# A two-layer graph-attention kernel: unroll factor 4 to 8, a power in place of Newton steps, and a second attention with transposed scores, fp32 probabilities in column tiles and a mask added by TensorE

## The chip, the cores and the metric

The kernel runs on one core of one Trainium2 chip. The metric is the device time of one execution in microseconds. The core has TensorE (PE for its matmuls, PEld for its weight loads), VectorE (DVE), ScalarE (ACT), GpSimd (POOL) and SyncE (SP, which issues the transfers). Each engine runs its own list of instructions and waits for the others on semaphores.

## What is computed

64 graphs (batches) of 256 nodes with 256 features each go through two graph-attention layers with 8 heads of 32 dimensions. Cut to what matters:

```
# layer 0
q, k = src @ Wq + bq, src @ Wk + bk
attn = softmax(q @ k.T / sqrt(32))                      # per head
out = sum over r in 0..3 of (attn * (adj == r)) @ (src @ Wv[r] + bv[r])
x = layernorm(src + out @ Wo + bo)                      # g1, beta1
x = layernorm(x + gelu(x @ W1 + b1) @ W2 + b2)          # the feed-forward
# layer 1
q, k, v = x @ Wq, x @ Wk, x @ Wv
e = q @ k.T ; e = where(e >= 0, e, 0.2 * e)             # per head, leaky
attn = softmax(where(adj > 0, e, -9e15))
h = layernorm(attn @ v)
out = layernorm(concat(h, x) @ Wffn.T) + x
```

A row of `adj` without any edge has all its scores at -9e15, so its softmax is uniform.

## The kernel before

A batch is two tiles of 128 nodes. The kernel has three stages, one after the other, each with a barrier at its end and with its results in DRAM: `attention_first` (names with `a_`), `feed_forward` (`f_`, on pairs of batches) and the second attention, `attention_layer` with layer 1 (`l_`). Between the first two stands a general form of layer 0, which runs only where `adj` has values other than 0 and 1.

**How a stage is ordered.** The engines' lists are written by hand as a software pipeline. `run_steps` (L68) calls `step(t)` for one batch after the other: first 2·U of them written out, then a loop `Fori(2, B // U)` (L74) whose body holds U batches, then a tail. U is 4, so eight batches are written out and the loop runs 14 times four. The feed-forward does the same with pairs (L1644), in 6 loop passes. A step has eight slots, one for each head; a table `AT` says in which slot, counted from the batch's first, each part of a batch's work is put, so that a step holds work of several batches at once. Where two parts fall into one slot, the order of the code in `step` decides.

**First attention.** It forms the transposed scores and needs no transposes of P. Per batch: projections with fp16 high and low parts (three products for each, L1456 to L1458), store of q and k to a scratch in DRAM and six loads into a `stack` whose 96 rows hold the three high/low combinations, the scores (L1485) for the row maxima, the maxima turned and stored and loaded as two more rows of the stack (98 rows), transposed scores with the maximum already subtracted (L1472), the exponential on ScalarE (L1211) to fp32 `prob`, and value products in fp32 whose results, 32 rows each, lie in four column tiles of TensorE at once (L1547, L1550). Per batch, one turn of the negative maxima stands on TensorE (L1558). GpSimd makes the low part `a_xl` of the next input (L1303) after ScalarE's high part `a_xh` (L1227), and the low part `a_hl` of the heads (L1294), for which TensorE's output projection waits. The layernorm's reciprocal root is, after the variance, a seed on VectorE (with the negated mean five small operations) and three Newton steps of four operations on [128 x 2] on GpSimd (L1323), then the shift (L1326).

**Second attention.** Per head and batch: TensorE makes the scores (L909) and adds the mask, a bf16 product with the identity (L912), for each of the two node tiles; ScalarE makes the leaky part (a relu scaled by 4, L473, one pass of 512 columns), VectorE joins it with the scores and finds the row maximum in the same pass (L726, two of 256 columns), ScalarE makes the exponentials with their row sums (L433, two of 256), TensorE transposes the fp32 P (L896, four), ScalarE copies its high part (L446), VectorE subtracts for the low part (L732), and TensorE multiplies with the values in twelve products of 32 columns (L813 to L815). Around the heads stand the projections, `l_qk` with its low parts (L698), its store and eight loads into `l_stack` for each batch, two layernorms by the same Newton steps, and the output projection, copied to `l_y` (L792).

## Time and profile before

| | |
|---|---|
| median of three runs | 3583.69 us |
| the three runs | 3582.01 to 3592.45 us |
| the profiled execution | 3597.16 us |
| its span | 3594.9 us |
| first attention | 0 to 1244 us |
| feed-forward | 1244 to 1990 us |
| second attention | 1990 to 3595 us |
| busy share of the span | TensorE 86% (weight loads 64%), VectorE 76%, ScalarE 68%, GpSimd 49% |
| mean granted clock of TensorE | 0.944 of full speed |

The profile is of one execution. The stage borders are where the names of the instructions change. An engine's busy share over the span is a mean over three stages with different limits, so the views below are taken by stage. TensorE's records overlap, since a matmul enters the engine while the one before leaves it: the distance from one start to the next tells what a matmul costs, its own duration doesn't. PEclk is the granted clock as a share of full speed. The queue rows (PEldq, SPq) are control instructions, as the branch at a loop's end.

### The profile page before, as it was taken

The page shows a single profiled execution, that of the slowest core. Times are in us where ns is not written, and L with a number is a line of the kernel's source. Part 1 is how long each engine was busy: PE and PEld are TensorE (multiplying, and loading weights), DVE is VectorE, ACT ScalarE, POOL GpSimd, SP SyncE. Part 2 cuts the span into 40 slices and gives each one's busy share as a digit, 9 for nine tenths or more (in the row PEclk, how much of TensorE's full clock was granted, in tenths as well). Part 3 has the DMA queues.
Part 4 walks back from the last instruction along what each step waited for, and adds up shares of the span by engine and source line. Part 5 has one row for each costly group of instructions (what it writes and reads, how often), then busy time and mean ns, then how long its engine had stood idle before and what let it go on. Part 6 is the DMA issues. An engine that isn't in the chain of part 4 may idle for free. (4 is left out here: it accounts for less than half of the span.)

```text
span 3594.9 us, 96982 instructions
## 1 busy us (share of the span) xinstructions
PE 3085.4 (86%) x31169; PEld 2287.0 (64%) x31169; DVE 2723.2 (76%) x7645; ACT 2427.9 (68%) x5646; POOL 1769.1 (49%) x3716
## 2 busy tenths in 40 slices
PE   5999999999999489999999488878888888788886
PEld 3666666666665256666666377767777777677775
DVE  4888888888888345655555388888888888888886
ACT  2566666666666255555555488888888888888886
POOL 0566666666666425545545034443444444344445
PEclk9999999999999789999999699998999999999998
DMA  3444444444444111111111344443443444344332
GB/s 117 131 133 132 132 132 132 132 132 132 132 132 124 42 47 48 54 52 47 47 47 38 94 113 115 118 114 102 114 119 103 112 115 115 100 113 119 106 109 60
DMA packets 296923, 364.46 MB, mean 101 GB/s; under 512 B 29536, under 2 KB 213728, under 8 KB 296544
## 3 DMA queue, kind: packets, MB, share of 16 engines
q1 hardware_dynamic: 295104, 358.20, 33.6%
q8 instruction: 185, 3.03, 0.4%
q14 instruction: 194, 1.59, 0.2%
q10 hardware_dynamic: 1440, 1.65, 0.1%
HBM read 241.77 MB, written 117.96 MB: 100 GB/s over the span
## 5 line engine op out<-in xcount | busy, mean ns | idle before, releaser
L433 ACT ACTIVATE l_prob<-l_neg_e,l_neg_max 128x256 f32<-128x256 f32 x1024 | 518.0, 522 | 18.0 <-DVE l_neg_max L726 10.2
L726 DVE CUSTOM_DVE_ANT_0 l_neg_e<-l_score,l_leaky 128x256 f32<-128x256 f32 x1024 | 391.7, 420 | 151.0 <-ACT l_prob L433 93.1
L896 PE MATMUL l_tprob<-l_ident,l_prob 128*128 128x128 f32 x2048 | 362.3, 304 | 157.8 <-ACT l_prob L433 146.8
L473 ACT ACTIVATE l_leaky<-l_score 128x512 f32<-128x512 f32 x512 | 307.6, 601 | 219.8 <-PE l_score L912 219.6
L1774 DVE TENSOR_TENSOR f_gl<-f_act,f_gh 128x512 f16<-128x512 f32 x256 | 244.9, 957 | 275.5 <-ACT f_act L1701 275.4
L909 PE MATMUL l_score<-l_stack 128*128 128x256 f16 x1024 | 283.3, 299 | 107.0 <-DMA l_stack<-qk_scratch 106.9
L1696 ACT ACTIVATE f_gh<-f_up,f_b 128x512 f16<-128x512 f32 x256 | 175.5, 685 | 279.1 <-PE f_up L1822 279.0
L1387 DVE TENSOR_TENSOR a_linked<-a_prob,a_mask 128x1024 f32<-128x1024 f32 x256 | 350.2, 1368 | 6.9 <-ACT a_prob L1211 6.9
L732 DVE TENSOR_TENSOR l_pt<-l_tprob,l_pt 128x512 f16<-128x512 f32 x512 | 351.1, 686 | 1.4 <-ACT l_pt L446 1.4
L896 PEld LDWEIGHTS l_tprob<-l_ident,l_prob 128*128 128x128 f32 x2048 | 235.9, 151 | 174.7 <-ACT l_prob L433 130.2
L543 POOL TENSOR_TENSOR l_hl<-l_zt,l_hh 128x512 f16<-128x512 f32 x64 | 74.0, 1156 | 507.6 <-ACT l_hh L493 507.6
L1380 DVE TENSOR_REDUCE a_neg_max<-a_score 128x4 f32<-128x1024 f32 x256 | 307.3, 1200 | 4.1 <-PE a_score L1485 4.1
L1211 ACT ACTIVATE a_prob<-a_score_t 128x1024 f32<-128x1024 f32 x256 | 259.6, 1014 | 74.9 <-PE a_score_t L1472 73.4
L446 ACT ACTIVATE l_pt<-l_tprob 128x512 f16<-128x512 f32 x512 | 309.0, 604 | 1.0 <-PE l_tprob L896 1.0
L912 PE MATMUL l_score<-l_mask,l_identb 128*128 128x256 bf16 x1024 | 283.7, 299 | 0.0
L1820 PE MATMUL f_down<-f_w,f_gh 128*128 128x256 f16 x1024 | 279.2, 273 | 1.0 <-DVE f_gl L1774 1.0
L1822 PE MATMUL f_down<-f_w,f_gl 128*128 128x256 f16 x1024 | 279.1, 273 | 0.0
L1821 PE MATMUL f_down<-f_w,f_gh 128*128 128x256 f16 x1024 | 279.1, 273 | 0.0
L1432 DVE SCALAR_TENSOR_TENSOR a_qk<-a_proj,a_vcol,a_qk 128x256 f16<-128x256 f32 x256 | 112.1, 480 | 144.6 <-ACT a_qk L1220 144.5
L814 PE MATMUL l_heads<-l_vl,l_pt 128*128 128x32 f16 x2048 | 208.5, 178 | 12.1 <-issue 12.1
L433 ACT ACTIVATION_READ_ACCUMULATOR l_prob<-l_neg_e,l_neg_max 128x1 f32 x1024 | 218.2, 213 | 0.0
L813 PE MATMUL l_heads<-l_vh,l_pt 128*128 128x32 f16 x2048 | 211.3, 179 | 0.8 <-DVE l_pt L732 0.8
(227 smaller groups left out, 10376.2 us busy)
## 6 DMA issues: line engine op xcount, KB each, us to landing
l_stack<-qk_scratch SPq DMA_DIRECT2D x512, 128.0 KB, 3.1
a_stack<-qk_scratch SPq DMA_DIRECT2D x384, 128.0 KB, 2.8
qk_scratch<-a_qk SPq DMA_DIRECT2D x64, 512.0 KB, 2.8
qk_scratch<-l_qk SPq DMA_DIRECT2D x64, 512.0 KB, 4.7
a_x_sb<-x_t SPq DMA_DIRECT2D x64, 256.0 KB, 2.7
a_adj_sb<-adj_t SPq DMA_DIRECT2D x64, 256.0 KB, 2.8
a_res<-x_nodes SPq DMA_DIRECT2D x64, 256.0 KB, 3.0
after_attention<-a_z_out SPq DMA_DIRECT2D x64, 256.0 KB, 2.1
```

Source lines behind the costliest of these rows:

```text
L433: last = nc.scalar.activation(prob[:, s, i], src[:, i], ACT.Exp, bias=neg_max[:, s, i:i + 1], scale=1.0 if first else -1.0, accum_out=rsum ...
L446: nc.scalar.activation(pt[:, ht % PTB, 0], tprob[s][:], ACT.Copy).then_inc(pt_high, 1)
L473: nc.scalar.activation(leaky4[:, s], score[s][:], ACT.Relu, scale=1.0 / ALPHA - 1.0).then_inc(relu_done, 1)
L726: last = nc.vector.tensor_tensor_reduce(neg_e[:, s, i], score[s][:, i], leaky4[:, s, i], -ALPHA, 3e38, ALU.add, ALU.min, neg_max[:, s, i:i ...
L732: nc.vector.tensor_tensor(pt[:, ht % PTB, 1], tprob[s][:], pt[:, ht % PTB, 0], ALU.subtract).then_inc(pt_low, 1)
L896: last = nc.tensor.transpose(tprob[s][:, jt, it * P:(it + 1) * P], prob[:, s, it, jt * P:(jt + 1) * P], ident[:])
L909: last = nc.tensor.matmul(score[s][:, it], stack[:, i, 0, a, c * N + it * P:c * N + (it + 1) * P], stack[:, i, 1, a, c * N:(c + 1) * N], s ...
L912: last = nc.tensor.matmul(score[s][:, it], identb[:], mask[:, i, it * N:(it + 1) * N], start=False, stop=True)
L1380: nc.vector.tensor_reduce(neg_max[:, i, 0:MROWS].rearrange("p (a c t) -> p c a t", a=HQ, c=DC)[:, c, a0:a0 + 2], score[:], AX_X, ALU.max, ...
L1387: nc.vector.tensor_tensor(linked[:, k], prob[:, k], mask[:, be[1] % 2].unsqueeze(1).to_broadcast([P, 2, NT * N]), ALU.mult).then_inc(link_ ...
L1820: nc.tensor.matmul(out, lhs_h, rhs_h, start=start, stop=False)
L1821: nc.tensor.matmul(out, lhs_h, rhs_l, start=False, stop=False)
```

## The change

1. **U from 4 to 8.** 16 batches (or pairs) are written out ahead of each loop, the body holds 8, and the loop runs 6 times (2 times in the feed-forward). `attention_first` keeps its four buffers by a constant of its own, so its waits and transfers keep their distances.
2. **The reciprocal root** in all stages: VectorE makes only var + eps and the negated mean (three small operations fewer), GpSimd raises to -0.5 (one operation on [128 x 2]) and makes the shift. The wait that guards the root's buffer moves from VectorE to GpSimd.
3. **A new second attention**, `attention_second` (names with `b_`), built like the first:
   - The scores of each head are made twice. Once as before with the mask added (one bf16 product of 512 columns), only for the row maximum, which VectorE takes in one plain pass of 512 columns.
   - Once transposed, in PSUM `score_t`: two products of 256 columns; ScalarE replaces them in place by 4·relu; TensorE adds the mask `far` times 5·(-9e15) (one bf16 product of 512 columns) and the scores once more, this time with the two rows that subtract the maximum (two products of 256); ScalarE makes exp(0.2·x) in one pass of 512 columns to fp32 `prob`, which lies already as the values need it.
   - Values and sums by fp32 products in four column tiles, as in the first attention. The sums are turned and inverted by VectorE.
   - The maximum goes through one transpose, two small VectorE operations, a store and a load per batch.
   - Nodes without edges: `linked` (VectorE, from the transposed adjacency), a count by TensorE, `any_link` (VectorE), `zero_q` (VectorE, one product over q's both parts, 1024 columns), `far` (GpSimd). Both forms of the adjacency are loaded for each batch, 256 KB each, where there was one.
   - The x-part of the output projection (`out_x`) runs on the kept `xh`, `xl`; layernorm's scale and shift are folded into the weights and one row, so the output is `y = bank + out_row`.

```diff
-U = 4
-RSQRT_MAGIC = float(0x5F3759DF)
-NEWTON = 3
+U = 8
...
-                        n = 0
-                        for _ in range(NEWTON):
-                            for out, a, c, op in ((s["prod"], s["half"], s["root"], ALU.mult), (s["prod"], s["prod"], s["root"], ALU.mult),
-                                                  (s["prod"], s["prod"], three_halves, ALU.add), (s["root"], s["root"], s["prod"], ALU.mult)):
-                                nc.gpsimd.tensor_tensor(out[:], a[:], c[:], op).then_inc(root_chain, 1)
-                                n += 1
-                                pool.wait_ge(root_chain, count(bg, ROOTS, n))
+                        if (n := after(back(bg, 1), 1, 1)) is not None:
+                            pool.wait_ge(z_ready, n)
+                        nc.gpsimd.tensor_tensor(s["root"][:], s["var"][:], minus_halves[:], ALU.pow).then_inc(root_chain, 1)
+                        pool.wait_ge(root_chain, count(bg, ROOTS, 1))
                         nc.gpsimd.tensor_tensor(shift[:], s["neg_mean"][:], s["root"][:], ALU.mult).then_inc(root_chain, 1)
...
+def attention_second(nc, x_in, x_out, adj, adj_t, w, scr, scr_m, consts):
...
+    AT = {"load": 4, "load_adj": 4, "xT": 8, "xh": 9, "xl": 9, "q": 10, "q_hi": 11, "q_lo": 11, "linked": 8, "k": 12, "k_hi": 13, "k_lo": 13,
+          "count": 9, "any": 9, "v": 14, "v_out": 15, "zero_q": 12, "far": 10, "store_qk": 13, "mask": 16, "S": 17, "max": 17,
+          "offset": 24, "turn_max": 25, "max_rows": 26, "store_m": 26, "ST": 28, "relu": 28, "add": 29, "exp": 29, "values": 33, "res": 45,
+          "evac": 40, "turn_sum": 40, "rinv": 41, "turn_heads": 43, "hs": 43, "stats0": 44, "z1": 45, "turn_z": 46, "hh": 46, "hl": 47,
+          "out_x": 47, "out": 48, "y": 49, "stats1": 50, "z": 52, "affine": 53, "store": 55}
...
+                        sp.dma_start(scr[i].rearrange("k p n -> p k n"), qk[:, i]).then_inc(qk_stored[i], 16)
+                        sp.wait_ge(qk_stored[i], parts_stored)
...
+                        for blk, (kq, kk) in enumerate(((0, 2), (1, 2), (0, 3))):
+                            for which, kind in ((0, kq), (1, kk)):
+                                sp.dma_start(stack[DH * blk:DH * (blk + 1), r4, which],
+                                             scr[i, kind].rearrange("(a r) n -> r a n", r=DH)).then_inc(stack_loaded[r4], 16)
...
+                        act.wait_ge(added, head_count(be, he))
+                        if he % HQ == 0 and (n := after(back(be, 1), HALVES, 2 * (he // HQ) + 2)) is not None:
+                            act.wait_ge(values_done, n)
+                        nc.scalar.activation(prob[:, he], score_t[s][:].rearrange("p t n -> p (t n)"), ACT.Exp,
+                                             scale=ALPHA).then_inc(exp_done, 1)
...
+                        act.wait_ge(scores_t_done, head_count(br, hr))
+                        nc.scalar.activation(score_t[s][:], score_t[s][:], ACT.Relu, scale=SLOPE - 1.0).then_inc(relu_done, 1)
...
+                        nc.vector.tensor_reduce(neg_max[:, i, col:col + NT], score[s][:], AX_X, ALU.max, negate=True).then_inc(max_done, 1)
...
+                        pe.wait_ge(relu_done, head_count(be, he))
+                        if he == 0:
+                            pe.wait_ge(max_loaded[r4], uses(be, RING) * 16)
+                            pe.wait_ge(far_ready, count(be, 1, 1))
+                        nc.tensor.matmul(score_t[s][:].rearrange("p t n -> p (t n)"), far_ident[:], far[:, r4].rearrange("p t n -> p (t n)"),
+                                         start=False, stop=False, skip_group_check=True)
+                        for jt in range(NT):
+                            last = nc.tensor.matmul(score_t[s][:, jt], stack[0:KS, r4, 1, a, c * N + jt * P:c * N + (jt + 1) * P],
+                                                    stack[0:KS, r4, 0, a, c * N:(c + 1) * N], start=False, stop=True, skip_group_check=True)
+                        last.then_inc(added, 1)
...
+                        for term in range(2):
+                            for a in range(HQ):
+                                he = HQ * c + a
+                                part = slice(DH * a, DH * (a + 1))
+                                if term:
+                                    last = nc.tensor.matmul(sums_t[part, 0:N], pick[:, c], prob[:, he, cols], start=k == 0, stop=k == 3)
+                                else:
+                                    nc.tensor.matmul(heads_t[part, c], values[:, r4, jt, he * DH:(he + 1) * DH], prob[:, he, cols],
+                                                     start=jt == 0, stop=jt == 1)
...
-    attention_layer(nc, 1, mid2, out, adj, w1, scr1, consts)
+    attention_second(nc, mid2, out, adj, adj_t, w1, scr1, scr_m, consts)
```

**What stands on TensorE for a head of the second attention, before.** In one slot of the loop: `l_tprob` takes the transposed P of one head, `l_score` the scores and mask of a later head, and `l_heads` the values of an earlier one (four rounds of three, two shown).

```order
L896 MATMUL l_tprob<-l_ident,l_prob 128x128 x4
L909 MATMUL l_score<-l_stack 128x256
L912 MATMUL l_score<-l_mask,l_identb 128x256
L909 MATMUL l_score<-l_stack 128x256
L912 MATMUL l_score<-l_mask,l_identb 128x256
L813 MATMUL l_heads<-l_vh,l_pt 128x32
L814 MATMUL l_heads<-l_vl,l_pt 128x32
L815 MATMUL l_heads<-l_vh,l_pt 128x32
L813 MATMUL l_heads<-l_vh,l_pt 128x32
L814 MATMUL l_heads<-l_vl,l_pt 128x32
L815 MATMUL l_heads<-l_vh,l_pt 128x32
```

After, in one slot, with the buffer numbers: `b_score_t0` is completed for one head, `b_score_t1` begun for the next, `b_score0` made for the maximum of a later batch; `b_back_bank` holds turned maxima and the count.

```order
L2091 MATMUL b_score_t0<-b_far,b_far_ident 128x512
L2094 MATMUL b_score_t0<-b_stack 128x256 x2
L2103 MATMUL b_score_t1<-b_stack 128x256 x2
L2113 REGISTER_ALU
L2115 MATMUL b_score0<-b_stack 128x256 x2
L2117 MATMUL b_score0<-b_mask,b_identb 128x512
L2187 MATMUL b_back_bank<-b_ident,b_offset 128x128
L2190 REGISTER_ALU
L2194 MATMUL b_back_bank<-b_linked,b_ones 128x256 x2
L2214 MATMUL b_heads_t<-b_prob,b_values 32x256 x4
L2212 MATMUL b_sums_t<-b_prob,b_pick 32x256 x4
```

The transposes of P are gone. The second addition into `b_score_t0` stands first in the slot and waits for ScalarE's relu of a product that was issued one slot earlier; the products of the next head's `b_score_t1` stand right behind it. One quarter of a batch's values stands in every other slot.

**What stands on GpSimd in the first attention before `a_xl`, before.** The last of the three Newton steps, the shift and the low part of the next input:

```order
L1323 TENSOR_TENSOR a_nw_prod<-a_nw_half,a_nw_root 128x2
L1323 TENSOR_TENSOR a_nw_prod<-a_nw_prod,a_nw_root 128x2
L1323 TENSOR_TENSOR a_nw_prod<-a_nw_prod,a_three_halves 128x2
L1323 TENSOR_TENSOR a_nw_root<-a_nw_root,a_nw_prod 128x2
L1326 TENSOR_TENSOR a_shift<-a_nw_neg_mean,a_nw_root 128x2
L1303 TENSOR_TENSOR a_xl<-a_x_sb,a_xh 128x512
```

After:

```order
L1303 TENSOR_TENSOR a_nw_root<-a_nw_var,a_minus_halves 128x2
L1305 TENSOR_TENSOR a_shift<-a_nw_neg_mean,a_nw_root 128x2
L1285 TENSOR_TENSOR a_xl<-a_x_sb,a_xh 128x512
```

One power stands where twelve operations stood; `a_xl` and what follows it, up to `a_hl`, keep their order.

## Rows read from the trace of the kernel before

**Rows 1.** Stages: us; busy PE, PEld, DVE, ACT, POOL (xcount); PEclk; DMA share; GB/s.

```profile
0.00:1244.00 1244.00, 1123.90 (x11713) 706.49 (x11713) 1012.33 (x1747) 698.82 (x1285) 762.44 (x1284) 0.99 0.40 124
1244.00:1990.00 746.00, 699.25 (x4864) 479.49 (x4864) 414.47 (x899) 419.17 (x707) 354.88 (x512) 0.97 0.15 49
1990.00:3595.00 1605.00, 1262.26 (x14592) 1101.00 (x14592) 1296.36 (x4999) 1309.93 (x3654) 651.79 (x1920) 0.90 0.39 108
```

**Rows 2.** One line's instructions: count: least/mean/most ns, first to last start; shapes.

```profile
L1558 PE MATMUL a_sums_t<-a_ident,a_neg_max x53: 327/328/332, 215.4 to 1149.3; 128*128 128x128 f32 x53
...
L792 DVE COPY l_y<-l_back_bank x4: 680/680/681, 2281.2 to 2350.0; 128x512 f32<-128x512 f32 x4
...
L792 DVE COPY l_y<-l_back_bank x49: 678/680/682, 2281.2 to 3441.9; 128x512 f32<-128x512 f32 x49
...
L1485 PE MATMUL a_score<-a_stack x1024: 270/272/422, 45.4 to 1173.3; 96*128 96x256 f16 x171
```

**Rows 3.** Loop branches on TensorE's queue, in the three stages; columns as before.

```profile
L74 PEldq COMPARE_BRANCH  x14: 76/208/234, 209.9 to 1143.8; - x14
...
L1644 PEldq COMPARE_BRANCH  x6: 76/208/230, 1504.7 to 1939.0; - x6
...
L74 PEldq COMPARE_BRANCH  x13: 3469/3819/3950, 2262.5 to 3422.7; - x13
```

**Rows 4.** Timeline of two first-attention batches: start us, us, engine, line, [idle <-releaser].

```profile
598.84 0.62 ACT L1227 ACTIVATE a_xh<-a_x_sb 128x512 f16<-128x512 f32 x1
...
599.62 1.16 POOL L1303 TENSOR_TENSOR a_xl<-a_x_sb,a_xh 128x512 f16<-128x512 f32 x1
...
613.47 0.20 POOL L1323 TENSOR_TENSOR a_nw_prod<-a_nw_half,a_nw_root 128x2 f32<-128x2 f32 x1 [1.43 <-DVE a_nw_root L1425]
...
616.45 0.62 ACT L1227 ACTIVATE a_xh<-a_x_sb 128x512 f16<-128x512 f32 x1
...
617.33 0.20 POOL L1323 TENSOR_TENSOR a_nw_root<-a_nw_root,a_nw_prod 128x2 f32<-128x2 f32 x1
...
617.77 1.17 POOL L1303 TENSOR_TENSOR a_xl<-a_x_sb,a_xh 128x512 f16<-128x512 f32 x1
```

**Rows 5.** Waits, 200:1100 and 2200:3400: engine, its work <- releaser: us, times, longest.

```profile
PEld a_back_bank L1456 <- POOL a_hl L1294: 50.3, 50, 1.4
...
PE l_score L909 <- DMA l_stack<-qk_scratch: 80.0, 45, 2.5
```

**Rows 6.** Timeline of TensorE in the first attention, columns as in rows 4.

```profile
600.77 0.66 PE L1563 MATMUL a_back_bank<-a_ident,a_rinv_wide 128*128 128x128 f32 x4
601.26 0.60 PE L1472 MATMUL a_score_t<-a_stack 98*128 98x256 f16 x4
601.70 0.38 PE L1456 MATMUL a_proj<-a_wn,a_xh 128*128 128x512 f16 x1
601.92 0.38 PE L1457 MATMUL a_proj<-a_wn,a_xh 128*128 128x512 f16 x1
...
603.00 0.60 PE L1485 MATMUL a_score<-a_stack 96*128 96x256 f16 x4
603.53 0.64 PE L1550 MATMUL a_heads_t<-a_prob,a_values 128*32 128x256 f32 x8
...
604.42 0.61 PE L1547 MATMUL a_sums_t<-a_prob,a_pick 128*32 128x256 f32 x8
604.97 0.61 PE L1472 MATMUL a_score_t<-a_stack 98*128 98x256 f16 x4
```

**Rows 7.** Group by shape, 2200:3400: xcount | busy us, mean ns | idle before.

```profile
L473 ACT ACTIVATE l_leaky<-l_score 128x512 f32<-128x512 f32 x397 | 238.1, 600 | 170.3 <-PE l_score L912 170.2
```

**Rows 8.** DMA issues of the whole run: xcount, KB each, median us to landing.

```profile
l_stack<-qk_scratch SPq DMA_DIRECT2D x512, 128.0 KB, 3.1
...
qk_scratch<-a_qk SPq DMA_DIRECT2D x64, 512.0 KB, 2.8
qk_scratch<-l_qk SPq DMA_DIRECT2D x64, 512.0 KB, 4.7
```

More of the change, by code:

```diff
@@ L78, in run_steps, with norm_scratch @@
         step((B // U + r // U, r % U))
-def newton_scratch(ctx, nc, name, n):
-    return {k: ctx.enter_context(nc.sbuf_tensor(f"{name}_{k}", [P, n], I32 if k == "bits" else F32))
-            for k in ("var", "half", "bits", "root", "prod", "neg_mean")}
+def norm_scratch(ctx, nc, name, n):
+    return {k: ctx.enter_context(nc.sbuf_tensor(f"{name}_{k}", [P, n], F32)) for k in ("var", "root", "neg_mean")}
 def attention_layer(nc, layer, x_in, x_out, adj, w, scr, consts, other_edges=None, general=False):
@@ L204, in attention_layer @@
         shift = [sb(f"shift{i}", [P, NT], F32) for i in range(2)]
-        nw = [newton_scratch(ctx, nc, f"{L}nw{i}", NT) for i in range(2)]
+        nw = [norm_scratch(ctx, nc, f"{L}nw{i}", NT) for i in range(2)]
         score = [psum(f"score{i}", [P, NT, N]) for i in range(2)]
@@ L1065, in attention_first @@
         prep = sem("prep")
-        x_loaded = [sem(f"x_loaded{i}") for i in range(U)]
+        x_loaded = [sem(f"x_loaded{i}") for i in range(XS)]
         adj_loaded = [sem(f"adj_loaded{i}") for i in range(2)]
@@ L1134, in step @@
                     if bx := due(t, h, "load"):
-                        i = bx[1] % U
-                        if (n := after(back(bx, U), 1, 1)) is not None:
+                        i = bx[1] % XS
+                        if (n := after(back(bx, XS), 1, 1)) is not None:
                             sp.wait_ge(xl_ready, n)
@@ L1582, in feed_forward @@
     FC = FF // P
-    ROOTS = 4 * NEWTON + 1
-    SEEDS = 4
+    ROOTS = 2
+    SEEDS = 2
     LOW = 8
@@ L1747, in step @@
                     pool.wait_ge(seed_chain, count(bd, SEEDS, SEEDS))
-                    n = 0
                     s = nw
-                    for _ in range(NEWTON):
-                        for out, a, c, op in ((s["prod"], s["half"], s["root"], ALU.mult), (s["prod"], s["prod"], s["root"], ALU.mult),
-                                              (s["prod"], s["prod"], three_halves, ALU.add), (s["root"], s["root"], s["prod"], ALU.mult)):
-                            nc.gpsimd.tensor_tensor(out[:], a[:], c[:], op).then_inc(root_chain, 1)
-                            n += 1
-                            pool.wait_ge(root_chain, count(bd, ROOTS, n))
+                    if (n := after(back(bd, 1), 1, 1)) is not None:
+                        pool.wait_ge(z_ready, n)
+                    nc.gpsimd.tensor_tensor(s["root"][:], s["var"][:], minus_halves[:], ALU.pow).then_inc(root_chain, 1)
+                    pool.wait_ge(root_chain, count(bd, ROOTS, 1))
                     nc.gpsimd.tensor_tensor(shift[:], s["neg_mean"][:], s["root"][:], ALU.mult).then_inc(root_chain, 1)
```

688 lines of the change are left out of this document (633 added, 55 removed).

## The prediction, made before the changed kernel ran

> **What bounds the kernel now.** I read the stages first [rows 1]: the first attention takes 1244 us, the feed-forward 746, the second attention 1605, and the profiled run is 3597.2. The program is three pipelines one after another, so a stage's gain is the kernel's gain. In the first attention TensorE is busy 90% of the whole stage, start and end included, at clock 0.99; in the feed-forward 94%. In the second attention TensorE is busy 79%, VectorE 81% and ScalarE 82%, at clock 0.90: no engine is full there, they wait for each other. Then I read the rhythm [rows 2]. The turn of the maxima in the first attention comes 53 times in 933.9 us: one batch each 17.96 us, across twelve loop ends and more. In the second attention three periods inside one pass of the loop take 68.8 us (22.9 each), but 48 periods across twelve loop ends take 1160.7 us. 48 × 22.9 would be 1101, so **each return to the loop's head costs some 5.0 us there**. The cause is on TensorE's queue [rows 3]: the branch itself takes 0.21 us in the first attention and in the feed-forward, and 3.8 us in the second. The loop bodies have four batches (four pairs in the feed-forward). By the matmul counts of [rows 1], 11713 / 64, 4864 / 32 and 14592 / 64, and a weight load for each matmul, a body has 1460, 1220 and 1820 TensorE instructions. Somewhere between 1460 and 1820 the return becomes dear.
>
> **Part 1: U from 4 to 8.** All bodies double: about 2930 in the first attention, 2430 in the feed-forward, and 8 × 205 × 2 = 3280 in the new second attention (205 matmuls from the code: 64 in the heads, 60 projections, 64 for values, since each fp32 product stands in the trace twice, 15 transposes, 2 of the count). All three are now past the dear end. Fori(2, 8) returns five times, Fori(2, 4) of the feed-forward once. Cost: first attention 5 × 5.0 = **+25 us**, feed-forward **+5**. Bounds: the branch alone, 3.6 × 6 = 22, and twice the 5.0 where TensorE is full, 60; I keep 30, the only case that the trace has. The second attention returned 13 times (65 us); now 5 times, 25 us, counted in part 3. The Trainium skill ("Runtime: NRT & Kernel Launch", section "Instruction fetch mechanics") says that TensorE holds 2048 instructions and that a taken branch to a target outside what is held stalls on a fetch. It speaks against this part: by it, too, bodies of 2430 and 2930 stall where 1220 and 1460 did not. The trace agrees on both sides of that size, except that 1820 (with register and wait instructions some 1930) already stalls. Straight-line code is fetched in the first eight batches of each stage, and the first loop passes are no faster than those, so I price streaming at nothing; if it isn't, part 2's gain is gone.
>
> **Part 2: the reciprocal root.** Twelve small GpSimd steps and three of VectorE become one power. In the first attention these twelve run from 613.47 to 617.53, then the shift, and only then the low part of x at 617.77, while ScalarE had finished the high part at 616.45 + 0.62 = 617.07 [rows 4]. Behind that, GpSimd runs without a pause to the low half of the heads (hl), for which TensorE waits before the output projection: 50.3 us over 50 batches, 1.0 each [rows 5]. With the chain shortened GpSimd starts at 617.1, 0.7 us sooner. In the batch before, it started at 599.62 where the high part was done at 599.46, only 0.16 late [rows 4]. Mean 0.43 × 64 = **−27 us**. Neither a power nor its price is in the trace. Its bounds are 0.2 us (a product of this size, [rows 4]) and 3.5 (all that it replaces); up to about 3.3 us it makes no difference, since the high part of x comes later. Gain between 0 and the whole wait, 64. The wait that guards the root's buffer now stands on GpSimd, ahead of xl and hl, but it asks for the z of the batch before, which is due six slots earlier. In the feed-forward TensorE is full and nothing moves; in the second attention the step is off the path.
>
> **Part 3: the new second attention.** It is built like the first: TensorE becomes the bound, so I add up its work with the intervals of [rows 6]. Four 256-column products take 0.44 (0.11 each), one of 512 takes 0.22. A group of four column-tiled fp32 products takes 0.43 to 0.46 (two from 603.53 to 604.42), and entering and leaving fp32 costs 0.1 each (0.53 for a score group ahead of values, 0.55 for the last value group). Four transposes take 0.49.
> Each head: scores 2 × 0.11 + mask 0.22, transposed scores 0.22, their second addition 0.22 + 0.22: 1.09 × 8 = 8.7. Projections (q, k, v 36 and output 24 products): 6.5. Count 0.2. Values: four halves of two groups, 1.08 each: 4.3. Fifteen transposes: 2.1. Sum **21.8 us** per batch. The same sum for the first attention gives 17.0 where it takes 17.96, and the wait of part 2 is the difference. What leaves: 32 fp32 transposes of P and 96 narrow value products on TensorE, one copy and one subtraction of 512 columns per head, and the maximum fused with the leaky step. VectorE then has 8 plain maxima and about ten 512-column operations of 0.68 [rows 2]: under 16 us. ScalarE has sixteen of 0.60 [rows 7] for the heads and about 6 us of others: also under 16.
> What keeps it from 21.8 is waiting in TensorE's order. The longest path is k, its high and low parts, the store, six loads, the scores of the next slots. After k come 0.65 until the next addition is done, 1.0 and 0.6 on ScalarE, 0.7 on VectorE, a store of 2.8 us as in the first attention or 4.7 as here, about 2.8 for six issues (0.47 apart), and a landing of 3.1 [rows 8]: 11.7 to 13.6. TensorE has 12.3 us of other work between. So it waits 0 to 1.2 us per batch; now it waits 80.0 us in about 50 batches, 1.6 each [rows 5]. I take 0.6 for this and the smaller waits together, the middle, because this stage's transfers are the slow kind but the loads fall from eight to six: **22.4 us** per batch, 23.4 as the upper bound.
> The stage: 50 us to the first scores (45.4 in the first attention, [rows 2]), 64 × 22.4 = 1434, less 26 for the light first and last steps (the first attention's scores span 45.4 to 1173.3, 1127.9 us, where 64 × 17.96 would be 1149; 21 × 22.4 / 17.96), 78 behind the last scores (71 there, 1173.3 to 1244), and 25 for the returns: 1561 against 1605, **−44 us**.
>
> **Sum.** 3597.2 + 25 + 5 − 27 − 44 = 3556 for a profiled run. The median of the runs is 3583.7, 13.5 below the profiled one, so **3543 us**, 1.1% faster.
>
> **Rivals.** *The cover holds fully*: TensorE keeps to 21.8 and GpSimd frees 0.7 per batch: 38 and 18 us less, 3487. For it: the first attention, built alike, shows no wait but the one of part 2. Against: DMA completions are longer in this stage. *ScalarE closes a ring (slower)*: leaky step and exponential of a head now lie between two additions on TensorE, in place in the same bank. From the point where a slot's ring is longer than its TensorE work, the ring decides. Ring: 0.6 for the addition's end, 2 × 0.6, 0.2 of signals, 2.0 per slot, plus what ScalarE holds in the slot: 0.9, 0.6, 0, 0.6, 1.1, 1.7, 0.6, 0.6. TensorE's slots are 3.2, 2.5, 2.4, 2.6, 2.4, 2.1, 2.9, 3.4. The larger of the two each time: 3.2, 2.6, 2.4, 2.6, 3.1, 3.7, 2.9, 3.4 = 23.9. That is 1.5 more per batch than I take: 3543 + 96 = 3639. Against it: ScalarE does its other work while TensorE adds, so only slots 4 and 5 exceed, and the neighbours can absorb it. *The loops cost twice and GpSimd frees nothing*: TensorE refills slowly where it is full (+30) and hl stays late because VectorE stretches GpSimd's operations (+27): 3600.
>
> **How the numbers follow.** Forecast 3543 (own range 3515 to 3575) 0.45; cover holds 0.22; ring 0.15; loops and GpSimd 0.18. A difference under 0.3% (11 us) can't be told from none. Faster: 0.43 + 0.22 + 0.03 = 0.68. Same: 0.02 + 0.07 = 0.09. Slower: 0.15 + 0.08 = 0.23. Range 3485 to 3605: it leaves out the ring and the cheapest end.
>
> **What would show it.** TensorE's branch at 3.5 us and more in all three loops, 11 taken in all (right for part 1; if it stays at 0.2 in the first attention, 25 us are saved). GpSimd's xl begins as ScalarE's xh ends, and the wait for hl falls under 0.6 per batch. In the second attention TensorE is busy 95% or more at a clock near 1, one y each 22.4 us; waits named for the stack's DMA show the path of part 3, waits of the addition for relu show the ring. I am wrong if the first attention loses more than 15 us, or the second's period is over 23.4.

## The result, and the profile after

The changed kernel takes **3458.33 us** (median of four runs, 3450.32 to 3462.94), the kernel before in the same measurement 3584.81. The ratio is 0.9642, 95% interval 0.9617 to 0.9666: 3.6% faster, 126 us. The forecast was 3543 us, 1.1% faster, with a range of 3485 to 3605. The sign was right; the forecast gain was three times too small, and the time lies 27 us under the range.

The same three windows as [rows 1], of the changed kernel (columns as there):

```profile
0.00:1213.00 1213.00, 1114.15 (x11713) 703.52 (x11713) 999.61 (x1555) 690.40 (x1285) 599.80 (x580) 0.99 0.42 129
1213.00:1959.00 746.00, 700.33 (x4864) 479.73 (x4864) 402.84 (x803) 419.18 (x707) 285.69 (x160) 0.97 0.15 50
1959.00:3454.00 1495.00, 1396.63 (x12902) 991.44 (x13124) 914.03 (x2386) 900.02 (x1734) 427.71 (x512) 0.97 0.39 116
```

The first attention became 31 us shorter (forecast: 2), the feed-forward stayed as it was (forecast: 5 longer), and the second attention became 110 shorter (forecast: 44). Together 141, which is the difference of the two profiled runs (span 3594.9 and 3454.0). It is more than the 126 of the medians, because the profiled run of the kernel before lies 12 us over its median of 3584.8 and that of the changed kernel 3 under its own; a stage's time, read from one profiled run, carries such differences. In the second attention VectorE and ScalarE fell from 81% and 82% to 61% and 60%, TensorE rose from 79% to 93% of the stage, its clock from 0.90 to 0.97.

The branches at the loops' ends on TensorE's queue, first attention, feed-forward, second attention, against [rows 3] (count: least/median/most ns, first to last start; the last branch of each loop isn't taken and takes 0.08 us):

```profile
L72 PEldq COMPARE_BRANCH  x6: 83/3684/4049, 414.3 to 1130.0; - x6
...
L2305 PEldq COMPARE_BRANCH  x2: 83/2440/4797, 1733.3 to 1911.2; - x2
...
L72 PEldq COMPARE_BRANCH  x6: 83/3919/4316, 2468.5 to 3351.5; - x6
```

As forecast, all three loops now return dearly. What the array itself loses is less. The timeline of TensorE around the second return of the first attention (start us, us, line, [idle before]):

```profile
558.75 0.27 PE L1430 MATMUL a_proj<-a_xh,a_wq 128*128 128x256 f16 x1
561.54 0.61 PE L1457 MATMUL a_score<-a_stack 96*128 96x256 f16 x4 [2.52 <-issue]
```

The branch is held from 557.2 for 4.05 us, but the matmuls queued ahead of it run until 559.02: 2.52 us of idle array.

The wait for the low half of the heads (against [rows 5]; 200 to 1100 us), and the new root on GpSimd:

```profile
PEld a_back_bank L1428 <- POOL a_hl L1276: 32.9, 46, 1.0
```

```profile
L1303 POOL TENSOR_TENSOR a_nw_root<-a_nw_var,a_minus_halves x50: 711/712/713, 210.9 to 1085.2; 128x2 f32<-128x2 f32 x50
```

The wait is 0.7 us per batch instead of 1.0 (the prediction named "under 0.6" as the sign of its reading), and the power costs 0.71 us. With the shift behind it, GpSimd is free again 1.0 us after the chain's start, where twelve operations and the shift took 4.3 [rows 4]. The next `a_xl` then waits for ScalarE's high part alone, as forecast.

The second attention's rhythm, against the rows of `l_y` in [rows 2]: seven outputs inside one pass of the loop, and the last of the 64:

```profile
L1975 DVE TENSOR_TENSOR b_y<-b_back_bank,b_out_row x7: 683/685/693, 2497.3 to 2627.5; 128x512 f32<-128x512 f32 x7
...
L1975 DVE TENSOR_TENSOR b_y<-b_back_bank,b_out_row x64: 683/691/693, 2083.9 to 3442.3; 128x512 f32<-128x512 f32 x64
```

130.2 / 6 = 21.7 us per batch with a hiccup of 0.3; most are 21.6. And the scores, for the two ends of the stage: they start 36 us behind 1959 and end 59 us before 3454.

```profile
L2115 PE MATMUL b_score<-b_stack x1024: 270/272/421, 1995.3 to 3395.2; 96*128 96x256 f16 x171
```

The waits of TensorE in the second attention (2100 to 3400 us for the first row, 2100 to 3300 for the second), against the 80.0 us of `l_stack` in [rows 5]:

```profile
PE b_score L2115 <- DMA b_stack<-qk_scratch: 1.8, 6, 0.7
```

```profile
PEld b_score_t L2091 <- ACT b_score_t L1827: 22.2, 54, 0.4
```

The stack comes in time. The second row is idle time of the weight loads, once in a batch, and the profile puts it down to the relu. In the batch at 2708 us that relu had ended at 2708.47 (2707.88 + 0.59), the load started at 2708.86, and the array had other matmuls until 2708.93: at this place TensorE lost nothing to the relu. The transfers of this stage became as short as those of the first ([rows 8] had 4.7 and 3.1):

```profile
b_stack<-qk_scratch SPq DMA_DIRECT2D x384, 128.0 KB, 2.9
...
qk_scratch<-b_qk SPq DMA_DIRECT2D x64, 512.0 KB, 2.9
```

### The profile page after: what moved, and what is told of

Read it like the earlier page. It is cut to its first block and busy times, and to the rows that moved or that the text cites. A ratio compares the mean times of both kernels' runs of the same rounds, so it can differ in the third digit from the quotient of the medians.

```text
span 3454.0 us, 81387 instructions
## 1 busy us (share of the span) xinstructions
PE 3211.1 (93%) x29479; PEld 2174.7 (63%) x29701; DVE 2316.5 (67%) x4744; ACT 2009.6 (58%) x3726; POOL 1313.2 (38%) x1252
## 5 line engine op out<-in xcount | busy, mean ns | idle before, releaser
L1821 ACT ACTIVATE b_prob<-b_score_t 128x512 f32<-128x512 f32 x512 | 304.0, 594 | 457.1 <-PE b_score_t L2094 457.1
L2009 DVE TENSOR_REDUCE b_neg_max<-b_score 128x2 f32<-128x512 f32 x512 | 352.2, 688 | 310.2 <-PE b_score L2117 265.4
L1827 ACT ACTIVATE b_score_t<-b_score_t 128x512 f32<-128x512 f32 x512 | 303.5, 593 | 0.7 <-PE b_score_t L2103 0.7
L2115 PE MATMUL b_score<-b_stack 96*128 96x256 f16 x1024 | 198.2, 276 | 17.2 <-DMA b_stack<-qk_scratch 16.9
L2094 PE MATMUL b_score_t<-b_stack 98*128 98x256 f16 x1024 | 197.4, 273 | 15.3 <-issue 10.5
L2471 PE MATMUL f_up<-f_xh,f_w 128*128 128x512 f16 x512 | 195.3, 381 | 5.9 <-DVE f_xl L2447 3.4
L2103 PE MATMUL b_score_t<-b_stack 96*128 96x256 f16 x1024 | 196.8, 273 | 0.0
L2472 PE MATMUL f_up<-f_xl,f_w 128*128 128x512 f16 x512 | 195.3, 381 | 0.0
L2473 PE MATMUL f_up<-f_xh,f_w 128*128 128x512 f16 x512 | 195.1, 381 | 0.0
L2362 ACT ACTIVATE f_act<-f_up,f_b 128x512 f32<-128x512 f32 x256 | 173.8, 679 | 0.0
L2117 PE MATMUL b_score<-b_mask,b_identb 128*128 128x512 bf16 x446 | 173.2, 388 | 0.0
```

Source lines behind the costliest of these rows:

```text
L1821: nc.scalar.activation(prob[:, he], score_t[s][:].rearrange("p t n -> p (t n)"), ACT.Exp, scale=ALPHA).then_inc(exp_done, 1)
L1827: nc.scalar.activation(score_t[s][:], score_t[s][:], ACT.Relu, scale=SLOPE - 1.0).then_inc(relu_done, 1)
L2009: nc.vector.tensor_reduce(neg_max[:, i, col:col + NT], score[s][:], AX_X, ALU.max, negate=True).then_inc(max_done, 1)
L2094: last = nc.tensor.matmul(score_t[s][:, jt], stack[0:KS, r4, 1, a, c * N + jt * P:c * N + (jt + 1) * P], stack[0:KS, r4, 0, a, c * N:(c + ...
L2103: last = nc.tensor.matmul(score_t[s][:, jt], stack[0:KQ, r4, 1, a, c * N + jt * P:c * N + (jt + 1) * P], stack[0:KQ, r4, 0, a, c * N:(c + ...
L2115: last = nc.tensor.matmul(score[s][:, it], stack[0:KQ, r4, 0, a, c * N + it * P:c * N + (it + 1) * P], stack[0:KQ, r4, 1, a, c * N:(c + 1) ...
```

## The experiments

Eight further kernels ran. Six stand in this table, with the kernel before and the changed one; the other two are the changed kernel with one instruction issued twice, and follow below. The first four rows make a ladder from before to after, the others go beyond:

| kernel | median us | ratio to before (95%) | profiled stages, us |
|---|---|---|---|
| before | 3584.8 to 3587.6 | | 1244 / 746 / 1605 |
| power alone (U 4, old second) | 3544.69 | 0.9876 (0.9859 to 0.9893) | 1213 / 743 / 1594 |
| power and U 8, old second | 3496.17 | 0.9743 (0.9727 to 0.9759) | 1216 / 749 / 1530 |
| changed kernel | 3458.33 | 0.9642 (0.9617 to 0.9666) | 1213 / 746 / 1495 |
| U 4, 4, 8 | 3442.00 | 0.9596 (0.9580 to 0.9612) | 1208 / 742 / 1491 |
| U 4, 4, second written out | 3425.77 | 0.9546 (0.9530 to 0.9562) | 1211 / 742 / 1472 |
| same with the old second | 3437.64 | 0.9589 (0.9573 to 0.9605) | 1215 / 743 / 1492 |
| all written out | 3415.69 | 0.9525 (0.9509 to 0.9541) | 1205 / 741 / 1470 |

(The stages are windows of one profiled run each, cut where the names change. Four of these kernels have the same first attention, with the power and U 4; it took 1213, 1208, 1211 and 1215 us. So a few us in one stage can't be told from none.)

### The power alone

```diff
-U = 8
+U = 4
...
-    attention_second(nc, mid2, out, adj, adj_t, w1, scr1, scr_m, consts)
+    attention_layer(nc, 1, mid2, out, adj, w1, scr1, consts)
```

(against the changed kernel; against the one before, only the power is new)

> Part 2 alone: the power in place of the Newton steps in all stages, U 4, the old second attention. The chain theory: in the full stretch of the first attention TensorE no longer waits 0.7 us for the low half of the heads in every other batch, 64 x 0.4 = 26 us; at its end, where nothing hides the chain of GpSimd, the four gaps ahead of the last output projections shrink as they did in the changed kernel, 12 us; the end of the feed-forward 4 us; start and second attention some 5. Together 45 to 50 us, near 3537 us. The rival, that these ends got shorter because of U 8 or of the new second attention and that the power only fills a hidden place, expects at most 26 us and 3558 or more.

Measured: 3544.69 us, 43 less than the kernel before in the same measurement. The stages gave 31, 3 and 11:

```profile
0.00:1213.00 1213.00, 1118.94 (x11713) 704.47 (x11713) 997.61 (x1555) 691.41 (x1285) 601.52 (x580) 0.98 0.41 127
1213.00:1956.00 743.00, 698.94 (x4864) 479.48 (x4864) 402.41 (x803) 419.74 (x707) 284.24 (x160) 0.97 0.15 49
1956.00:3550.00 1594.00, 1260.46 (x14592) 1100.04 (x14592) 1184.03 (x4615) 1310.73 (x3654) 430.71 (x512) 0.90 0.39 109
```

The rival is refuted: the gain is well over the 26 us that the full stretch can give, with U 4 and the old second attention. In the full stretch itself the turns of the maxima stand 937.8 / 53 = 17.69 us apart, against 17.96 in [rows 2]: 17 us, not 26.

```profile
L1530 PE MATMUL a_sums_t<-a_ident,a_neg_max x54: 327/329/331, 210.6 to 1148.4; 128*128 128x128 f32 x54
```

In the drain of the first attention the waits for the heads' low half were, before (1160 to 1240 us) and with the power alone (1160 to 1212 us):

```profile
PEld a_back_bank L1456 <- POOL a_hl L1294: 19.9, 5, 6.6
```

```profile
PEld a_back_bank L1428 <- POOL a_hl L1276: 10.8, 3, 4.4
```

9 us of the 31 come from there. One batch after the other runs out, and GpSimd's chain is then all that TensorE has to wait for. The remaining 5 lie in the fill, ahead of the first turns, and are not shown to be the power's: the first turn comes at 58.1 us instead of 61.9, but in the four kernels with this same stage it comes anywhere from 56.2 to 61.0. Of the 11 us in the second attention 8 lie between its first and its last output (1477.6 us instead of 1485.5) and 3 behind them; no run shows by what path the power gave them.

### The power and U 8, with the old second attention

```diff
-    attention_second(nc, mid2, out, adj, adj_t, w1, scr1, scr_m, consts)
+    attention_layer(nc, 1, mid2, out, adj, w1, scr1, consts)
```

> Parts 1 and 2 with the old second attention. First attention and feed-forward as in the changed kernel (1213 and 746 us). The second attention has 5 returns to the loop's head for 13. If a return costs there the 5.0 us that the prediction took, its stage falls by 40 us to some 1560, and the median to some 3510. If a return costs only what it cost in the changed kernel (2.3 to 4.5 us), the stage falls by 18 to 30 us and the median is 3520 to 3532. What is left between this kernel and the changed one (3458) is the work of part 3 itself: 50 to 75 us.

Measured: 3496.17 us, below both expectations.

```profile
1965.00:3495.00 1530.00, 1230.39 (x14592) 1074.40 (x14592) 1179.91 (x4615) 1302.91 (x3654) 430.75 (x512) 0.93 0.40 113
```

Eight returns fewer took 64 us from the second attention: **8.0 us each**, not 5.0. (U also sets the number of this stage's input buffers, now eight instead of four. That is not what gave it: the same stage written out with four buffers, below, gains more.) So neither number was right for the old stage, and the theory had to change. The outputs `l_y` of this kernel come 21.5 and 22.7 us apart in turn through its sixteen written-out batches. The four-batch body of the kernel before never got back to their mean of 22.1: the period with a return is 28.1 us on average, some 6 more at once, and the three others of a pass, 22.9 on average [rows 2], were still those of a disturbed pipeline. The prediction took them for the undisturbed rhythm.

### The changed kernel with U 4, 4 and 8

```diff
+def staged(u, stage, *a, **k):
+    global U
+    U = u
+    stage(*a, **k)
...
-    XB = U
+    XB = 8
...
-    feed_forward(nc, mid1, mid2, wf, consts)
-    attention_second(nc, mid2, out, adj, adj_t, w1, scr1, scr_m, consts)
+    staged(4, feed_forward, nc, mid1, mid2, wf, consts)
+    staged(8, attention_second, nc, mid2, out, adj, adj_t, w1, scr1, scr_m, consts)
```

(the first attention likewise with 4)

> The changed kernel with U 4 in the first attention and in the feed-forward and U 8 only in the second attention. If the doubled body is what costs there, five gaps of 2.0 to 2.5 us in the first attention and one of 4.2 us in the feed-forward go: 16 us, 3442 us, with branches of 0.2 us on TensorE's queue. If the gaps come from something else, or the smaller bodies lose it elsewhere, the time stays at 3455 to 3460.

Measured: 3442.00 us, 16 less than the changed kernel, as expected. The branches of the first attention are cheap again:

```profile
L72 PEldq COMPARE_BRANCH  x14: 76/208/234, 202.6 to 1124.5; - x14
```

The doubled bodies of the first two stages are a loss of their own. It was some 10 us in the profiled stages (5 and 4), 16 in the medians. That the 16 met the expectation is in part chance: the intervals of the two ratios are only 0.0005 apart, and from the first to the last turn of the maxima the first attention takes 1103.6 us instead of 1109.1.

### The second attention written out

```diff
-    with eng.Fori(2, B // U) as q:
-        for r in range(U):
-            step((q, r))
+    if B // U > 2:
+        with eng.Fori(2, B // U) as q:
+            for r in range(U):
+                step((q, r))
...
+    staged(32, attention_second, nc, mid2, out, adj, adj_t, w1, scr1, scr_m, consts)
```

> As the kernel with 4, 4 and 8, but with the second attention written out without a loop. If only a taken branch stalls and straight code is fetched in time, its five returns (17 us together) go too: 3425 us, with 21.6 us per batch throughout. If straight code is fetched too slowly for TensorE beyond the first batches, the period rises over 21.8 us and the time is 3442 or more.

Measured: 3425.77 us. The outputs of 55 batches without a loop (2100 to 3300 us), and the stage:

```profile
L1976 DVE TENSOR_TENSOR b_y<-b_back_bank,b_out_row x55: 682/692/693, 2116.9 to 3282.8; 128x512 f32<-128x512 f32 x55
```

```profile
1953.00:3425.00 1472.00, 1385.10 (x12902) 988.27 (x13124) 912.40 (x2386) 900.49 (x1734) 427.35 (x512) 0.98 0.39 117
```

1165.9 / 54 = 21.59 us per batch to the end: straight code costs nothing here. Against the stage with five returns 19 us are gone, 3.8 per return; by the medians 16, 3.2 per return.

### The old second attention written out

The same, with `attention_layer` for the second stage and its four input buffers kept by constants (`XS = 4`, `XB = 4`).

> The kernel with 4, 4 and the second attention written out, but with the old second attention (and the power). New theory: undisturbed, the old second attention takes 22.1 us per batch (21.5 and 22.7 in turn, as in its first steps), and the 24.1 on average were the returns with what they leave behind, 8.3 us each. Then its stage takes some 1484 us and the kernel 3440, only 15 us more than with the new second attention written out (3426). The prediction's reading, 22.9 us per batch and 5.0 per return, gives 1525 us for the stage and some 3482.

Measured: 3437.64 us, against 3440 of the new theory and 3482 of the prediction's reading.

```profile
L775 DVE COPY l_y<-l_back_bank x54: 678/680/682, 2129.5 to 3303.9; 128x512 f32<-128x512 f32 x54
```

```profile
1958.00:3450.00 1492.00, 1217.20 (x14592) 1068.18 (x14592) 1176.51 (x4615) 1299.84 (x3654) 430.19 (x512) 0.94 0.40 116
```

1174.4 / 53 = 22.16 us per batch. From 1594 to 1492 us the thirteen returns were worth 102 us, 7.8 each (by the medians 107, 8.2 each), and with U 8 five cost 38, 7.6 each. The new second attention without returns is only 0.57 us per batch faster, 36 us over 64; 16 of these go to its longer start (its first output comes 120 us into the stage, the old one's at 104), and 20 are left in the profiled stages. The profiled run of the kernel with the old one, 3451.10 us, lies 13 over its median, so the medians are the better measure of the pair: 12 us (0.9546 against 0.9589; the intervals just don't meet).

These 0.57 us per batch go with the granted clock. Four windows of 22 us, about a batch each, in the old second attention written out:

```profile
2100.00:2122.00 22.00, 19.06 (x225) 16.79 (x226) 17.92 (x72) 19.61 (x56) 6.06 (x9) 0.92 0.40 111
2122.00:2144.00 22.00, 18.63 (x234) 16.42 (x231) 18.62 (x73) 20.57 (x62) 7.20 (x9) 1.00 0.46 129
2144.00:2166.00 22.00, 18.81 (x225) 16.58 (x224) 17.72 (x72) 19.62 (x56) 6.06 (x9) 0.92 0.42 110
2166.00:2188.00 22.00, 18.62 (x235) 16.57 (x233) 18.69 (x73) 20.56 (x60) 7.18 (x9) 1.00 0.45 128
```

Of its first 60 periods 30 hold a fall to 1.2 GHz, for 3 to 4 us, in or just ahead of them, and they take 22.5 to 23.4 us, 22.8 on average; the 30 others take 21.5 to 21.8, on average 21.55. The new second attention takes 21.59. From 2100 to 3300 us, the kernel before, the old second attention with U 8, written out, and the new one written out:

```profile
2100.00:3300.00 1200.00, 978.53 (x11402) 857.33 (x11401) 1010.41 (x3901) 1019.36 (x2852) 510.07 (x1502) 0.92 0.40 112
2100.00:3300.00 1200.00, 997.49 (x11973) 875.17 (x11972) 963.15 (x3778) 1063.66 (x2992) 352.93 (x419) 0.95 0.41 116
2100.00:3300.00 1200.00, 1018.40 (x12339) 898.48 (x12340) 990.38 (x3900) 1094.06 (x3086) 364.26 (x434) 0.96 0.42 120
2100.00:3300.00 1200.00, 1183.57 (x11205) 853.22 (x11397) 781.30 (x2059) 778.27 (x1503) 373.65 (x448) 1.00 0.41 124
```

In the third of these TensorE is busy 85% with pauses of up to 1.95 us, in the last 99% with none over 0.2. At full clock both second attentions take the same time per batch; the new one keeps its clock, the old one loses it in every other batch even where nothing returns. That the clock makes the difference is argued from these rows: no run held it fixed.

### The mask product twice

```diff
+                        nc.tensor.matmul(score_t[s][:].rearrange("p t n -> p (t n)"), far_ident[:], far[:, r4].rearrange("p t n -> p (t n)"),
+                                         start=False, stop=False, skip_group_check=True)
```

> The changed kernel with the mask product of the transposed scores issued twice (far_ident x far, one more bf16 product of 512 columns for each head). If TensorE is the bound of the second attention, each costs its 0.22 us in full: 8 x 64 x 0.22 = 113 us, 3571 us, 23.3 us per batch. If the ring through ScalarE or the path of k is what sets the period, part of it is hidden: 0 to 60 us.

Measured: 3567.50 us, 109 more than the changed kernel (expected 113 if TensorE is the bound). Seven outputs inside one pass:

```profile
L1975 DVE TENSOR_TENSOR b_y<-b_back_bank,b_out_row x7: 682/684/692, 2537.5 to 2677.3; 128x512 f32<-128x512 f32 x7
```

139.8 / 6 = 23.3 us. None of the added columns is hidden: TensorE sets the period here.

### The relu twice

```diff
-                        nc.scalar.activation(score_t[s][:], score_t[s][:], ACT.Relu, scale=SLOPE - 1.0).then_inc(relu_done, 1)
+                        nc.scalar.activation(score_t[s][:], score_t[s][:], ACT.Relu, scale=SLOPE - 1.0).then_inc(relu_first, 1)
+                        act.wait_ge(relu_first, head_count(br, hr))
+                        nc.scalar.activation(score_t[s][:], score_t[s][:], ACT.Relu).then_inc(relu_done, 1)
```

> The changed kernel with a second relu behind the first on the same bank: 0.65 us more between TensorE's two additions for each head, 5.2 us more of ScalarE per batch. If ScalarE closes the ring (the slower rival), every head pays: 8 x 64 x 0.65 = 333 us. If the slack read from the trace of the changed kernel holds (0.3 to 1.3 us between the relu's end and the next addition), only the heads with less than 0.65 pay the rest: 0.3 to 1.2 us per batch, 20 to 80 us in all.

Measured: 3508.41 us, 50 more: 0.8 us per batch where 5.2 were added. Seven outputs inside one pass, 133.7 / 6 = 22.3 us apart:

```profile
L1978 DVE TENSOR_TENSOR b_y<-b_back_bank,b_out_row x7: 683/684/693, 2515.5 to 2649.2; 128x512 f32<-128x512 f32 x7
```

The ring does not set the period, but it is near. In the changed kernel its tightest place is the slot in which ScalarE also makes the high part of k and the first layernorm's scaling (timeline of ScalarE and TensorE):

```profile
2709.31 0.38 PE L2103 MATMUL b_score_t<-b_stack 96*128 96x256 f16 x2
...
2709.34 1.09 ACT L1859 ACTIVATE b_z<-b_hs,b_shift,b_nw_root 128x256 f32<-128x256 f32 x2 [0.35 <-POOL b_shift L1890]
2710.33 0.58 ACT L1821 ACTIVATE b_prob<-b_score_t 128x512 f32<-128x512 f32 x1
2710.81 0.58 ACT L1827 ACTIVATE b_score_t<-b_score_t 128x512 f32<-128x512 f32 x1
...
2711.71 0.38 PE L2091 MATMUL b_score_t<-b_far,b_far_ident 128*128 128x512 bf16 x1
```

The relu ends at 2711.39, the addition starts 0.32 us later. In the kernel with the relu twice the additions that wait for it start 0.06 us after its end, so this head has some 0.26 us of slack. One other head starts its addition 0.39 to 0.47 us after the relu, the rest 0.67 and more. Against the added 0.65 us the first two, and by a little two others, are short by 0.7 us in sum, which is what the period grew by.

### All three stages written out

`staged(32, attention_first, ...)`, `staged(16, feed_forward, ...)`, `staged(32, attention_second, ...)`, no loop left.

> All three stages written out. If only a taken branch to code that is no longer held costs, nothing is left to gain against the kernel with 4, 4 and the second attention written out: 3425 us within 5. If straight code costs where TensorE is full, the first attention rises over 1209 us and the feed-forward over 734.

Measured: 3415.69 us, 10 less than expected, and the fastest of all: 4.7% under the kernel before. The intervals of this ratio and of the one with 4, 4 and the second attention written out overlap, so the 10 us rest on the traces. The first attention needed 1205 us instead of 1211. Its turns of the maxima are 929.2 / 53 = 17.53 us apart:

```profile
L1531 PE MATMUL a_sums_t<-a_ident,a_neg_max x54: 327/328/331, 212.3 to 1141.5; 128*128 128x128 f32 x54
```

With U 4 three are 17.6 and one, the first of each pass, is 18.0, and TensorE waits there 0.75 us for the low half of the heads instead of 0.40. This holds for the first pass of a loop too, to which nothing has returned yet (in the changed kernel the period from 278.5 us is 18.0, its first taken branch stands at 414.3). So some 0.4 us belong to the start of a pass and not to the branch of 0.2 us; what causes them is open. Straight code costs nothing where TensorE is full either. The feed-forward took 741 us, 742 with its loop, so the expectation's bound of 734 for it was set too low to tell anything.

### What a return does to the clock

In the changed kernel, five windows of 15 us behind the five returns of the second attention:

```profile
2468.00:2483.00 15.00, 12.81 (x128) 9.08 (x129) 8.49 (x24) 7.25 (x15) 1.46 (x4) 1.00 0.28 76
2644.00:2659.00 15.00, 12.54 (x106) 8.79 (x100) 7.04 (x21) 5.44 (x12) 0.00 (x0) 0.89 0.27 75
2821.00:2836.00 15.00, 12.68 (x127) 8.95 (x121) 8.35 (x24) 7.01 (x14) 1.31 (x4) 1.00 0.28 76
2997.00:3012.00 15.00, 12.39 (x103) 8.76 (x98) 7.09 (x21) 5.55 (x12) 0.00 (x0) 0.89 0.27 75
3174.00:3189.00 15.00, 12.86 (x107) 9.01 (x107) 7.36 (x22) 5.76 (x12) 0.13 (x1) 0.89 0.28 75
```

Where the granted clock stays at 1.00 the period with the return is 23.9 or 24.1 us, 2.3 to 2.5 over the 21.6 of the others. Where it falls to 0.89 in the mean of these 15 us (1.2 GHz for 3 to 4 of them) the period is 25.9, 26.1 and 25.5, 3.9 to 4.5 over. All five stalls of the array are 2.1 to 2.6 us long. So a return costs its stall, and in three of five cases about as much again at half clock. The first attention's five returns, with 2.0 to 2.5 us of idle array, leave the clock at 1.00. In the kernel before, the 18 us behind each of the thirteen returns have a mean clock of 0.81 (once 0.72). Behind the first, and ahead of it:

```profile
2262.00:2280.00 18.00, 14.15 (x151) 12.36 (x150) 12.45 (x47) 12.61 (x36) 5.16 (x7) 0.81 0.25 71
...
2240.00:2258.00 18.00, 14.20 (x188) 12.61 (x187) 15.59 (x56) 15.76 (x44) 7.47 (x17) 1.00 0.50 134
```

The same busy time holds 151 matmuls instead of 188, and VectorE and ScalarE, which were busy 87%, fall to 70%. In a stage where three engines are 80% full and wait for each other, nobody has the reserve to catch up. That last sentence is argued from these windows; no run took the clock's part and the waits' part from each other. Nor do all falls stand behind returns: from 2100 to 3300 us the clock is at 1.2 GHz for some 200 us in the kernel before and still for 92 in the old second attention without a loop.

## Why the prediction was wrong

For a profiled run the forecast was 3556 us, and the changed kernel's took 3456: 100 us less, of which the first attention has 29, the feed-forward 5 and the second attention 66. Between the medians 85 of them show, since the forecast took off 13.5 us for the step from a profiled run to the median, and here the profiled run lay 3 under it. The largest single step that failed is the 0.6 us per batch of waiting that part 3 put on top of its own sum; the next is the price of a return.

**The cost of a return (part 1), wrong both ways.** That the doubled bodies return dearly was right in all three loops, and the rule of the Trainium skill cited for it ("Runtime: NRT & Kernel Launch", section "Instruction fetch mechanics") came out the same way: the traces agree, with 3.3 to 4.8 us a branch where it was 0.2. They show the price by the size of the body, not what the queue does meanwhile. (The prediction's reading that the trace agreed "on both sides of that size" was wrong: the bodies of the kernel before have at most some 1930 instructions with waits, under 2048, so no row stood on the other side.) The price was taken from one stage and carried to others. In the first attention a return is 2.0 to 2.5 us, since the array works off what is queued: some 12 us for 25, and with the cheap starts of passes that U 4 has instead, 6 net. The feed-forward's single return cost 4.2 (5 forecast), given back by the power. In the second attention of the kernel before it was 7.8 us for 5.0 (8.2 by the medians), because 22.9 us per batch, read between two returns, was taken for the undisturbed rhythm, which is 22.2. The other bound of this part, 60 us in the full stages, is excluded: returning to U 4 there gave 16.

**The power (part 2), mechanism right, size too small.** Before, the turns of the maxima come 17.6 and 18.2 to 18.4 us apart in turn; with the power and U 4 they are 17.6, but for the first of a pass. So the 0.7 us of every other batch went as forecast, and the 0.16 us of the others did not. On average they fell by 0.27 us (17.96 to 17.69) where 0.43 was forecast, 17 us for 27; 0.1 of the missing part is the 0.4 us at the start of each pass, which now shows. Without any loop they are 17.53 us apart, and that this is just 0.43 less is chance, since 0.16 of it are the loops' share. What the working left out are the places outside the full stretch: the drain of the first attention gave 9 us, where nothing covers the chain, the feed-forward 3, and the second attention, "off the path", 11, which stay unexplained as do 5 in the first attention's fill. Together the power was worth 43 us by the medians instead of 27.

**The second attention (part 3).** Its own sum was good: 21.8 us per batch by intervals of the first attention, 21.6 measured, with TensorE as the bound (mask product twice). The step that failed is the 0.6 us of waiting added to it. The path of k took the low end: the store 2.9 us, not 4.7, the loads 2.9, and from 2100 to 3400 us the stack was waited for 1.8 us in all. 0.8 × 64 = 51 us of the error are here. The other terms of the stage: first scores after 36 us, not 50; last scores 59 us before the end, not 78; returns some 18, not 25; and the 26 us deducted for light first and last steps don't exist, as the scores span 1399.9 us, which is 64 × 21.6 and the returns. 1561 − 51 − 14 − 19 − 7 + 26 = 1496, measured 1495.

**Which part gave it.** By the ladder of the profiled runs: the power 45 us; U 8 another 55 (64 in the second attention, less 9 in the other two); the new second attention 41, of which 35 are in its stage. By the medians they are 43, 49 and 38. The forecast had 27 for the power; it booked U 8 as a loss of 30 and its gain of 40 within part 3, which left 4 for the new second attention itself. So the largest gain came from the part that was priced at 10 net, and by the medians of the written-out pair the new second attention is worth only 12 us once the returns are gone. Nowhere did the forecast price the clock: it read 0.90 in the second attention, and counted the new one at full clock without a term for what that would give.

**The rivals.** *The cover holds fully* was right on TensorE, which keeps to 21.6, and wrong on GpSimd, which freed 0.27 us per batch in the full stretch and not 0.7; its 3487 kept the overpriced returns (30 for 16) and the long ends. *ScalarE closes a ring* is refuted by the relu issued twice, 50 us for 333, though it named one right place, the slot that holds 1.7 us of other work of ScalarE. *The loops cost twice* is refuted. The range was too narrow below: its low end was one rival's centre, and two cheap ends could come true together.

## What to carry to other kernels

Read the undisturbed period of a loop where there is no loop: in the batches written out ahead of it. A period between two returns may still be recovering from the last. Choose the unroll factor for each stage by the number of TensorE instructions in its body, or write the stage out: here the one global factor won 64 us in one stage and lost 10 to 16 in two. Look at the granted clock of the undisturbed stretch before pricing a rewritten stage: part of what is gained may be that. And price a shortened chain a second time in the fill and the drain of each stage, where nothing hides it.

## What the hardware showed beyond that

- A taken branch on TensorE's queue is 0.21 us with some 1460 matmuls and weight loads in the body, and 3.3 to 4.8 us with 1820 and more (5.2 to 6.3 us in the feed-forward of three of the experiments). Nothing between 1460 and 1820 was tried. Straight code of 64 batches ran at 21.59 us per batch, so fetching in line costs nothing that the trace shows.
- In the second attention stalls of 2.1 to 2.6 us of the array are followed by half the clock in three cases of five, and not in the other two, at the same place of the same program; in the first attention of the same run stalls of 2.0 to 2.5 us never are. In the old second attention written out the clock falls in every other batch with no pause of the array over 1.95 us. Why is open.
- A power of [128 x 2] on GpSimd takes 0.70 to 0.71 us, as much as two and a half of the dependent products that it replaces (0.27 us from one to the next).
- The first batch of every loop pass takes some 0.4 us more in the full pipeline of the first attention, also in the first pass, which no taken branch leads to.
